# Three expert routes of a graph-and-FFN stack, rewritten: one running count, bf16 masks, one-hots with the node tile innermost

## The reference, cut to what matters

```python
# layer 1 ("sw"): one expert of 8, at most C = 489 nodes each; a node past that is dropped
logits = x @ gate_w + gate_b;  probs = softmax(logits);  idx = argmax(probs);  prb = probs[idx]
pos = (cumsum(one_hot(idx)) * one_hot(idx)).sum(-1) - 1;  kept = pos < C
y = expert_idx(x) * (prb * kept)
# layer 2 ("mo"): two experts of 8, weights = softmax of the two best logits
top_vals, top_idx = top_k(logits, 2);  w = softmax(top_vals);  y = sum_k w_k * expert_k(xn)
# layer 3 ("top"): one expert of 8, hidden rows H = gelu(x @ W1 + b1) are shared by all experts
assign = argmax(softmax(H @ Wg + bg));  y = probs[assign] * (H @ Wd[assign] + bd[assign])
```

## Time and profile before

| | |
|---|---|
| median of 3 runs | 3424.39 us (3424.29 to 3434.86) |
| the profiled execution | 3423.68 us, its span 3422.0 us |
| busy: PE, DVE, POOL, ACT | 2923.1, 2027.4, 2034.8, 1181.8 us |
| granted TensorE clock, mean of the span | 0.94 of full speed |
| sw route block and its first gathers | about 1836.5 to 1876.9 us of the span |
| mo route block and its first gathers | about 2497.3 to 2545.5 us |
| top route block and its first gathers | about 3230.6 to 3273.6 us |

### The profile page before, as it was taken

One profiled execution on the slowest core, in us unless ns is written; L12 is line 12 of the kernel. 1 busy time (PEld: TensorE's weight loads), 2 busy tenths in 40 slices (PEclk: granted clock), 3 DMA queues, 4 the chain that ended last, 5 costly groups with the idle time before them and its releaser, 6 DMA issues. The chain is left out here.

```text
span 3422.0 us, 49182 instructions
## 1 busy us (share of the span) xinstructions
PE 2923.1 (85%) x15083; PEld 2136.2 (62%) x15109; DVE 2027.4 (59%) x4867; ACT 1181.8 (35%) x2550; POOL 2034.8 (59%) x2061
## 2 busy tenths in 40 slices
PE   3887888898999999539994996999949979898788
PEld 3666667686555555329992664555739955457677
DVE  7766666984789899889995445100354444214532
ACT  4555553332222222459992222000223311103210
POOL 5777776765777777667675775577557722000064
PEclk9999999998999999769997998999979989999889
DMA  6555554102899998747654233654142254436253
GB/s 195 190 185 182 183 191 141 49 1 69 246 264 265 266 263 257 278 168 198 198 166 144 86 118 128 215 152 149 29 146 66 69 194 161 151 101 203 112 178 107
DMA packets 286322, 552.65 MB, mean 162 GB/s; under 512 B 63009, under 2 KB 181734, under 8 KB 285558
## 3 DMA queue, kind: packets, MB, share of 16 engines
q1 hardware_dynamic: 203238, 390.67, 34.5%
q0 software_dynamic: 82832, 158.84, 16.8%
HBM read 375.63 MB, written 174.69 MB: 161 GB/s over the span
## 5 line engine op out<-in xcount | busy, mean ns | idle before, releaser
L164 POOL DMA_INDIRECT edge_weights<-shares,share_cell x416 | 449.7, 1081 | 181.1 <-issue 78.2
L536 POOL DMA_INDIRECT layer_gnn_sum_rows<-xn_rows,src_cols x416 | 412.4, 991 | 155.2 <-issue 110.6
L155 POOL DMA_INDIRECT edge_counts<-repeats,count_cell x416 | 412.6, 992 | 142.4 <-issue 114.2
L1260 POOL DMA_INDIRECT xn_nodes<-gat_rows,src_cols x416 | 407.0, 978 | 148.9 <-issue 101.4
L1308 PE MATMUL bank<-layer_gnn_h_nodes,layer_gnn_s_onehot_t 128*128 x1664 | 485.0, 414 | 0.9 <-DVE layer_gnn_s_onehot_t L1329 0.2
L600 PE MATMUL bank<-layer_gnn_sum_onehot,layer_gnn_sum_rows 128*128 128x256 f32 x832 | 271.2, 409 | 85.8 <-DMA layer_gnn_sum_rows<-xn_rows,src_cols 79.3
L1308 PEld LDWEIGHTS bank<-layer_gnn_h_nodes,layer_gnn_s_onehot_t 128*128 128x128 f32 x1664 | 283.6, 190 | 79.9 <-issue 4.3
L1318 ACT ACTIVATE layer_gnn_s_enc<-bank 128x256 f32<-128x256 f32 x416 | 159.9, 384 | 401.7 <-PE bank L1301 398.9
L2890 PE MATMUL bank<-layer_gnn_b_weights,xn_nodes 128*128 128x391 f32 x768 | 255.2, 494 | 28.5 <-DMA layer_gnn_b_weights<-edge_weights 28.5
L1620 PE MATMUL bank<-layer_gnn_w_onehot,layer_gnn_w_part 128*128 128x256 f32 x832 | 250.6, 383 | 12.8 <-DVE layer_gnn_w_part L1665 12.2
L736 DVE TENSOR_TENSOR edge_sums_turned<-edge_sums_turned,bank 128x512 f32 x208 | 142.8, 687 | 153.7 <-PE bank L601 150.8
(11 more groups left out here) (660 smaller groups left out, 6135.4 us busy)
## 6 DMA issues: line engine op xcount, KB each, us to landing
kept_rows<-xn_nodes SPq DMA_DIRECT2D x104, 512.0 KB, 4.1
layer_gnn_w_rows<-kept_rows SPq DMA_DIRECT2D x104, 512.0 KB, 4.4
edge_weights<-layer_gnn_sum_zeros SPq DMA_DIRECT2D x108, 400.0 KB
layer_gnn_b_weights<-edge_weights SPq DMA_DIRECT2D x54, 782.0 KB, 4.4
layer_gnn_gcn_sum_counts<-edge_counts SPq DMA_DIRECT2D x50, 836.0 KB, 4.5
layer_gnn_s_dst_across<-in_dst_row SPq DMA_DIRECT2D x104, 256.0 KB
edge_counts<-layer_gnn_no_edges SPq DMA_DIRECT2D x25, 836.0 KB, 8.5
layer_ffn_e_w<-in_l1f_w SPq DMA_DIRECT2D x16, 1024.0 KB
```

Source lines behind the costliest of these rows:

```text
L155: nc.gpsimd.indirect_dma_start(g.counts, bass.IndirectOffsetOnAxis(ap=g.cell[:, sent(t):sent(t) + 1].bitcast(U32), axis=0), g.repeats[:, s ...
L164: nc.gpsimd.indirect_dma_start(g.weights, bass.IndirectOffsetOnAxis(ap=g.share_cell[:, sent(t):sent(t) + 1].bitcast(U32), axis=0), g.share ...
L536: nc.gpsimd.indirect_dma_start(rows[:, t % U, :], None, table, bass.IndirectOffsetOnAxis(ap=g.srcc[:, t:t + 1].bitcast(U32), axis=0)).then ...
L1260: nc.gpsimd.indirect_dma_start(rows[:, t % RING, :], None, htable, bass.IndirectOffsetOnAxis(ap=g.srcc[:, t:t + 1].bitcast(U32), axis=0)). ...
```

## The change

- **Masks.** A new `route_masks` runs on POOL in the gate block, ahead of the placements there (in top in a gate block where POOL had nothing to do). It makes bf16 masks in the layout [P, 8, 26], two [P, P] matrices for the counts and `places`, a [P, 128, 26] iota in bf16. DVE's wait for masks in the route block goes.
- **Counts.** Picks are bf16 [P, 8, 26]. One scan of 208 (reset at tile 0 by the mask `inside`) replaces the eight scans; two bf16 matmuls add into one bank (`later` holds 0 and -1, so that the bank has the count itself), and the bank is read directly.
- **Slots.** The float32 arithmetic of 26-wide steps is cut from 16 operations to 5 (sw) or 3 (mo, top) for a pick; the seven operations that found a tile's owner become a compare and a reduce, behind the one-hots.
- **One-hots.** `hot_tile`, `hot_place` and `sets` have the node tile innermost, all operands bf16 with unit step there; `hot_place` is made in two pieces (tiles 0 to 13, 14 to 25), and PE multiplies the first while the second is made. PE's operands `hot_place[:, :, t]` and `sets[:, :, t]` now step by 26 elements (52 bytes).
- **Gate weights.** The sum of the softmax goes to POOL (three additions, behind its placements). The weight parts' products, with 26 matmuls of their own into another bank, come after `take`.
- **First gathers in the route.** POOL issues the first four gathers of sw, and the first two of mo and top, in the route block as soon as `take` is there (and the row table, or the hidden rows, are stored). sw's first expert weights are loaded in the route block, behind the row table. The table's store is first on SP, as before.
- **Placements.** PLACED[6] 407 to 398 and COUNTED (112, 300, 336, 348, 370) to (98, 300, 338, 350, 364): 7 weights in the sw route in place of 16, 18 in the sw experts block in place of 9; counts 98 in the sw experts block (112), 240 in `weighted_products` (224), 12 in the mo gate (12), 14 in the mo route (22), 52 in the mo experts block (46).

```diff
-PLACED = (33, 141, 161, 185, 375, 391, 407)
-COUNTED = (112, 300, 336, 348, 370)
+PLACED = (33, 141, 161, 185, 375, 391, 398)
+COUNTED = (98, 300, 338, 350, 364)
@@ route, gpsimd
-            nc.gpsimd.iota(rev[:, :], ...)     # and six more masks
             if place is not None:
                 place(pool)
+            if r.weighs:
+                pool.wait_ge(expd, 1)
+                nc.gpsimd.tensor_tensor(halves[:, :, :], shown[:, 0:4, :], shown[:, 4:8, :], ALU.add).then_inc(summed, 1)
...
+            if begin is not None:
+                pool.wait_ge(taking, 1)
+                begin(pool)
@@ route, tensor
-            nc.tensor.matmul(g.ps[0][:, 0:NT * E], upto[:, :], every[:, :, :]..., start=True, stop=True)
-            nc.tensor.matmul(g.ps[1][:, 0:NT * E], g.ones[:, :], every[:, :, :]..., start=True, stop=True).then_inc(counted, 1)
+            nc.tensor.matmul(g.ps[0][:, 0:E * NT], r.later[:, :], flat(every), start=True, stop=False)
+            pe.wait_ge(ranked, 1)
+            last = nc.tensor.matmul(g.ps[0][:, 0:E * NT], r.all[:, :], flat(upto), start=False, stop=True)
...
+                for h, (lo, hi) in enumerate(PIECES):
+                    pe.wait_ge(placed_hot, 2 * k + h + 1)
+                    for t in range(lo, hi):
+                        last = nc.tensor.matmul(g.ps[2][:, 0:2 * T], hot_place[k][:, :, t], sets[k][:, 0:2 * T, t], ...)
+            last.then_inc(inverted, 1)
+            if r.weighs:
+                pe.wait_ge(weighed_hot, 3)
+                for t in range(NT):
+                    last = nc.tensor.matmul(g.ps[3][:, 0:3 * T], hot_place[0][:, :, t], sets[0][:, 2 * T:5 * T, t], ...)
@@ route, vector
+            nc.vector.tensor_tensor_scan(flat(upto), flat(r.inside), flat(every), 0.0, ALU.mult, ALU.add).then_inc(ranked, 1)
...
+                nc.vector.tensor_tensor(hot_tile[k][:, :, :], r.places[:, 1:T + 1, :], per_tile, ALU.is_equal).then_inc(hot, 1)
...
+                for lo, hi in PIECES:
+                    nc.vector.tensor_tensor(hot_place[k][:, :, lo:hi], r.places[:, 0:P, lo:hi], per_place[:, :, lo:hi], ALU.is_equal).then_inc(placed_hot, 1)
+            if r.weighs:
+                dve.wait_ge(summed, 3)
+                done(nc.vector.reciprocal(r.weight[:, 0, :], z[:, :]))
...
+            nc.vector.scalar_tensor_tensor(out=r.take[:, :], in0=raw[:, :], scalar=-float(P), in1=idle[:, :], ...).then_inc(taking, 1)
@@ new
+def route_masks(nc, r, pool):     # 5 iotas, of which places [P, P, NT]; 4 memsets; 2 selects; then waits for them
+    nc.gpsimd.iota(r.places[:, :, :], [[1, P], [0, NT]], base=0, ...).then_inc(r.masked, 1)
...
+            def take_first(pool):     # sw: four gathers; mo and top: two
+                pool.wait_ge(table_stored, 16)
+                take(0)
```

More of the change, by code:

```diff
@@ L1692, with route @@
     pass
-def route(nc, g, name, logits, picks, capacity, slots, r, src, table, place=None, meanwhile=None):
+def route(nc, g, name, logits, picks, capacity, slots, r, room, src=None, table=None, table_stored=None, place=None, meanwhile=None, begin=None, lent=()):
     with ExitStack() as stack:
@@ L1717, in route @@
-        wide = [P, NT, E]
-        rev, valid, number, upto = sb("_rev", [P, E]), sb("_valid", [P, NT]), sb("_number", [P, NT]), sb("_upto", [P, P])
-        best, first = [sb(f"_best{k}", [P, NT]) for k in range(2)], sb("_first", [P, NT])
-        pick = [sb(f"_pick{k}", wide) for k in range(picks)]
-        tmp, rest, every, cum, totals, incl = sb("_tmp", wide), sb("_rest", wide), sb("_every", wide), sb("_cum", wide), sb("_totals", wide), sb("_incl", wide)
-        zeros, ni, nf, ends = sb("_zeros", [P, NT]), sb("_ni", [P, E], I32), sb("_nf", [P, E]), sb("_ends", [P, E])
@@ L1801, in _ @@
+                    scores = rest[:, :, :]
             if picks == 2:
-                done(nc.vector.tensor_tensor(every[:, :, :], pick[0][:, :, :], pick[1][:, :, :], ALU.add))
-                nc.vector.tensor_tensor(z[:, :], best[1][:, :], best[0][:, :], ALU.subtract).then_inc(shifted, 1)
-            else:
-                done(nc.vector.tensor_copy(every[:, :, :], pick[0][:, :, :]))
-                nc.vector.tensor_tensor(tmp[:, :, :], logits[:, :, :], per_node(best[0]), ALU.subtract).then_inc(shifted, 1)
@@ L2252, in _ @@
             def _(pool):
-                def take(e):
-                    for n in range(NR):
-                        take_rows(nc, r, table, rows[:, e % 2, n, :], e * NR + n).then_inc(taken[e % 2], 16)
-                take(0)
                 take(1)
```

359 lines of the change are left out of this document (204 added, 155 removed).

## The result

| | before | changed kernel |
|---|---|---|
| median | 3426.44 us (4 runs, 3424.29 to 3434.86) | 3398.55 us (4 runs, 3393.66 to 3403.19) |
| ratio | 1 | 0.9914, 95% interval 0.9891 to 0.9936 |
| profiled execution, span | 3423.68, 3422.0 us | 3397.81, 3395.9 us |
| busy: PE, DVE, POOL, ACT | 2923.1, 2027.4, 2034.8, 1181.8 | 2946.9, 2001.1, 2051.2, 1181.9 |

By the ratio it is faster by about 29 us (27.9 between the medians, 26.1 between the two profiles); 52 were forecast. To find the rest I cut both profiles at the blocks' ends. Each engine closes a block with a DRAIN, then an event at which all meet; both are rows of the trace under the line where the block's stack closes. The lengths that follow are differences of DVE's closing events, so each block's length ends with the last engine that arrives.

What follows compares the result with a forecast made beforehand. DVE's chain in the route blocks was taken to bound the kernel. -18.6 (sw) - 21.9 (mo) - 15.5 (top) + 2.7 (`weighted_products`) + 0.6 (gates) = -52.7, from 3423.7 to 3371, median 3372 us; 8 in 10 between 3358 and 3392.

Steps and rivals of the forecast that it cites:

- Prices on DVE: DVE operations on bf16 tensors with unit step in the routes: half price, 0.26 us for 208 elements, 1.95 for 3328.
- Rival A: On DVE in the routes: no half price for two bf16 tensors, kernel at 3383 us; chance 0.16.
- sw, -18.6: sw route and experts: PE starts 15.6 us sooner, and the last scatter goes out 3 us earlier still.
- top, -15.5: top route: PE's second pair is turned at 27.5 us from the block's start, against 43.0 before.
- weighted_products, +2.7: `weighted_products`: 16 more placements take 20.8 us of POOL, which ends 3.1 us later than DVE, some 0.4 slack.
- mo, -21.9: mo route and experts: PE's first real work comes 26.3 us from the block's start, against 48.2 before.
- 21.6, 25, 26.3: mo route, us from the block's start: `take` at 21.6, block's end at 25, PE's first real work at 26.3.
- rival C: PE's strided reads in the routes: 0.30 us a matmul, not 0.14, kernel at 3381 us; chance 0.1.
- now the gather has landed when the block starts: Start of mo experts: only weight staging, turn and lift remain, 1.3 us before PE's first layer.
- The 6 counts more in the mo experts block: mo experts block: the added counts fall on tiles without gathers and cost 0.
- Gates, +0.6: sw and mo gates: masks of about 5.4 us on POOL add 0.3 us to each gate.
- D: sw and mo routes: POOL, slowed, keeps `take` waiting 5 us each, the change does half, 3382 us; chance 0.09.

Runs made afterwards that it cites:

- one_expert: Changed kernel with only the first expert's weights loaded in the sw route block, the second's at the experts block's start: 3393.80 us, ratio 0.9894.
- sum_early: Changed kernel with one expert's weights in sw's route, POOL's sum behind three of seven placements, top's first gathers in the experts block: 3397.27 us, ratio 0.9900.
- late_takes: Changed kernel with the first gathers of sw and mo back in the experts blocks, top left as it is: 3401.64 us, ratio 0.9910.
- counts_moved: Changed kernel with 236 counts in weighted_products (240), 4 in the mo gate (12), 64 in the mo experts block (52): 3406.07 us, ratio 0.9924.
- counts_0: Changed kernel with all 52 counts of the mo experts block placed in weighted_products instead: 3458.84 us in one execution.
- places_act: Changed kernel with `places` made by ACT at the start of each route block, not by POOL's iota in the gates: 3392.77 us, ratio 0.9883.
- before_again: The kernel before, unaltered, profiled once more: 3436.21 us in one execution.
- masks_last: Changed kernel with the masks made behind the placements, not ahead of them, in the sw and mo gates: 3397.83 us, ratio 0.9906.

## Why the prediction was wrong, step by step

- **Prices on DVE: right.** 0.27, 0.59, 0.92 and 1.95 us against 0.26, 0.58, 0.91 and 1.95; scan 0.59. Rival A is out. The Trainium skill (VectorE: DVE Perf Modes, The perf-mode tier table) has the double rate for `tensor_tensor` in bf16; the trace agrees (832 elements: 0.59 us). Operations that read [8, 26] across (reduces, the float32 steps on logits) took 0.50 to 0.58 where 0.37 to 0.41 were taken: 0.1 to 0.2 each.
- **sw, -18.6 against -16.4: nearly right.** `take` at 14.8 (13.6), PE at 26.0 (24.8), and 1.9 us more at the experts block's end (3). The tail was not "4 us to spare": the block ended at 25.4, held by the gathers' landing through POOL's DRAIN, as one_expert and sum_early show.
- **top, -15.5 against -14.2: right in its steps, with some luck in the number.** `take` at 13.0 (12.5), block end 20.9 (20), L2766 at 28.9 (27.5). The weights' 26 matmuls took 4.68 us, not 3.3. The experts block's 155.5 us is the shortest seen; twelve more profiles that gather early in top have 155.5 to 158.6, mostly 157.4, by which the gain would be about 12.3.
- **weighted_products, +2.7 against +0.9.** POOL last, DVE 1.3 us before it (3 was said). The 16 placements took 17.7 us of POOL, not 20.8. But this block varied from 342.2 to 346.3 us with the same placements, so neither number is confirmed.
- **mo, -21.9 against -11.5: the sum "21.6, 25, 26.3" and a term put at nothing failed, in three places.** (1) `take` at 24.9, 3.3 late: PE's pairs at 112 columns took 0.21 in place of 0.14, so that PE was still multiplying while "PE's last 12 matmuls" should have hidden (rival C's mechanism, at a price of about 2.6; the rest is the 0.1 to 0.2 us of the operations above). Two partial sums of the prediction are also added up wrongly (6.8 where it has 7.3, 5.6 for a pick where it has 5.3), but they cancel to within 0.1. (2) "now the gather has landed when the block starts" was true in the wrong way: the block does not start until it has landed. The first layer began 7.2 us behind `take`, not 4.7. Without the early gathers it was 6.4 (late_takes), so they account for 0.8 of these 2.5; in the kernel before it was 5.8, and 4.7 was too little either way. (3) "The 6 counts more in the mo experts block fall on tiles without gathers: 0." From its first layer to its end the block took 232.5 us after and 227.8 before, so 4.7 us of the earlier start were given back. 1.8 of them go with the early gathers (230.7 in late_takes), which leaves about 2.9 for the six more counts. That the counts lengthen this block is shown by counts_moved, where 12 more cost 12.4 us, and by counts_0 (225.7 from the first layer on). Together 3.3 + 2.5 + 4.7 = 10.5.
- **Gates, +0.6 against +10.1: the largest miss for its size.** The masks took 7.8 us, not 5.4: `places` was priced by a float32 row of another pattern (5.25 us, not 2.9). And "POOL sat idle for 3.71 us at the end of the sw gate and 5.38 of the mo gate, so bare they cost 1.7 and 0" read idle time as slack. It was the DRAIN: real slack was 1.6 us in sw, and none in mo. So mo paid 7.8, less 1.2 by which the DRAIN ended sooner behind the last issue (4.9 against 6.1), plus 0.2 of waits; sw paid 7.8 less 1.6 of slack and 2.7 of waiting for placements to land (3.15 before, 0.42 after). counts_moved and places_act show POOL as what held the gates.
- **Untouched blocks, 0 against +5.0.** Variation, by before_again.

2.2 + 1.3 - 1.8 + 10.4 + 9.5 + 5.0 = 26.6 us, all of the 52.7 - 26.1 that were missing. The range ended at 3392 and so held neither the gates nor the binding of mo's experts block: no rival had POOL at the end of a block, though D came near with POOL in front of `take`.

## What to carry to other kernels

An engine's idle time before a block's end is not slack until its closing DRAIN has been read: here POOL's DRAIN lasted until its indirect transfers had landed, so a transfer issued early for the next block also holds that block's start. Before work is moved onto an engine, ask of each block on its way whether that engine's closing comes last; the block-by-block table of closing events answers it in one look. Price an operation by a row of the same type and pattern, not only of the same size.

## What the runs showed of the hardware

- POOL's DRAIN at a block's end took 5 to 11 us by the profile (its start overlaps the last issues) and ended 2.8 to 6.9 us behind the issue of the last indirect DMA (sw gate 2.8, mo gate 4.9, sw route 6.1, in places_act 6.9), 0.5 us behind the landing of the last gather in the sw route; in masks_last, with nothing issued for 8 us, 1.6 us behind the last mask. The Trainium skill (VectorE: DVE Perf Modes, The DRAIN you can't avoid) gives the DRAINs of the preamble and postamble a constant of about 12 ns on all engines. DVE's at these block ends are 10 to 17 ns, like those; POOL's are not.
- PE reads a moving bf16 operand with a step of 52 bytes at 1.8 ns a column, at a granted clock of 0.89 as at 0.50 (4.53 and 4.55 us for 26 matmuls of 96 columns); a dense one takes 0.9 ns at the lower clock (2.17 us), and a strided stationary one costs at most 0.1 us a set (2.26).
- DVE and ACT write bf16 with a step of 224 bytes at 4.6 to 4.7 ns an element (6.71 and 6.85 us for 1456), over four times the 1.04 ns that DVE takes for dense elements in the earlier trace rows.
- POOL's iota cost 1.58 ns an element in the bf16 row (3328 elements, each number 26 times over) and 0.87 in the float32 row (3200 elements, a running count). The type alone is not shown to be the reason: a float32 iota at the kernel's start that repeats each number twice took 2.39 us for 416 elements (5.7 ns each).
